# Attention and fp8 feed-forward kernel: the order of work inside a half-group stage, with the output weights split first and the key projection ahead of the block products

## What is computed

```python
h = einsum('bct,bcd->bdt', x, W1[itok])
q, k, v = rope(h @ wq), rope(h @ wk), h @ wv        # 32, 8, 8 heads
out = softmax(mask(q k^T / sqrt(128))) v            # 4 query heads share a key head
x = x + out @ wo
y = einsum('bct,bcd->bdt', x, W2[itok])
x = x + fp8_round(fp8_round(y) @ fp8_round(qweight).T + bias)
```

## Time and profile before

| | us |
|---|---|
| median of 3 runs (lowest, highest) | 740.24 (737.14, 743.44) |
| the profiled execution | 742.31 |
| its span | 740.5 |
| busy in it: PE 587.3, DVE 433.7, POOL 319.0, ACT 250.3 | |

### The profile page before, as it was taken

The page is one execution under the profiler, slowest core; times in us unless marked ns, Lnnn a source line. Parts: engine busy times, 40 slices in busy tenths (PEclk is TensorE's granted clock), DMA queues, the critical chain, the costliest instruction groups (busy, mean ns, idle before and its releaser), DMA issues.

```text
span 740.5 us, 9212 instructions
## 1 busy us (share of the span) xinstructions
PE 587.3 (79%) x3150; PEld 465.9 (63%) x3150; DVE 433.7 (59%) x660; ACT 250.3 (34%) x477; POOL 319.0 (43%) x310
## 2 busy tenths in 40 slices
PE   8988985928993899668993899289948896798992
PEld 6866863827873687547772777268736775586840
DVE  5365768635566257724772467446652686367597
ACT  3331434340426033511442052404260335042253
POOL 2074886391267408470739043922664063230001
PEclk9999988768897879868995899788987898799997
DMA  7152120103010301030011201030102001200003
GB/s 257 57 185 86 57 86 0 43 2 113 1 42 1 114 0 42 0 113 0 0 42 43 70 0 42 0 113 0 42 0 71 15 1 60 72 15 1 1 0 113
DMA packets 32644, 35.27 MB, mean 48 GB/s; under 512 B 2251, under 2 KB 22859, under 8 KB 32620
## 3 DMA queue, kind: packets, MB, share of 16 engines
q1 hardware_dynamic: 32620, 34.96, 14.7%
HBM read 28.66 MB, written 6.29 MB: 47 GB/s over the span
## 4 chain that ended last, share of the span: by engine, by line
issue 37%; PE 29%; POOL 25%; DVE 6%; DMA 2%; ACT 1%; POOLq 1%; SPq 0%; DVEq 0%; ACTq 0%
POOL wq_lo L371 9%; POOL q_rot L385 7%; PE bank L724 6%; PE bank L725 5%; PE bank L726 5%; POOL wo_lo L380 4%; PE bank L784 3%; POOL k_rot L385 1%; DVE q_swap L1041 1%; DMA values<-v_st 1%; PE bank L696 1%; PE bank L667 1%; POOL w_sum L364 1%; PE bank L698 1%; PE bank L697 1%
## 5 line engine op out<-in xcount | busy, mean ns | idle before, releaser
L385 POOL TENSOR_TENSOR q_rot<-q_rot,q_swap 128x512 f32<-128x512 f32 x64 | 85.6, 1338 | 285.9 <-DVE q_swap L1041 285.9
L724 PE MATMUL bank<-wo_hi,o_hi 128*128 128x512 f32 x256 | 111.7, 436 | 103.7 <-POOL wo_lo L380 90.9
L1089 DVE TENSOR_TENSOR xacc<-xacc,bank 128x512 f32<-128x512 f32 x64 | 43.3, 677 | 149.4 <-PE bank L726 149.4
L724 PEld LDWEIGHTS bank<-wo_hi,o_hi 128*128 128x128 f32 x256 | 52.6, 205 | 122.9 <-issue 73.6
L531 ACT ACTIVATE o_hi<-bank 128x512 fp32r<-128x512 f32 x64 | 36.0, 598 | 233.9 <-PE bank L784 233.9
L725 PE MATMUL bank<-wo_lo,o_hi 128*128 128x512 f32 x256 | 107.4, 420 | 0.0
L726 PE MATMUL bank<-wo_hi,o_lo 128*128 128x512 f32 x256 | 107.1, 418 | 0.0
L514 ACT ACTIVATE q_swap<-bank 64x512 f32<-64x512 f32 x80 | 47.6, 596 | 108.7 <-DVE bank L1021 54.9
L784 PE MATMUL bank<-p_tr,v_st 32*128 32x128 f32 x512 | 57.6, 336 | 23.1 <-DVE s_nat L1047 11.6
L1041 DVE TENSOR_TENSOR q_swap<-q_swap,cst 128x512 f32<-128x512 f32 x80 | 72.4, 905 | 0.0
L784 PEld LDWEIGHTS bank<-p_tr,v_st 32*128 32x128 f32 x512 | 53.9, 232 | 29.2 <-issue 29.2
(11 more groups left out here) (161 smaller groups left out, 1095.1 us busy)
## 6 DMA issues: line engine op xcount, KB each, us to landing
raw_q<-in_L_attn_wq SPq DMA_DIRECT2D x16, 512.0 KB, 3.9
raw_o<-in_L_attn_wo SPq DMA_DIRECT2D x8, 1024.0 KB, 6.5
v_st<-values SPq DMA_DIRECT2D x16, 256.0 KB, 4.6
xacc<-in_x SPq DMA_DIRECT2D x4, 512.0 KB, 7.2
raw_k<-in_L_attn_wk SPq DMA_DIRECT2D x8, 256.0 KB, 4.3
values<-v_st SPq DMA_DIRECT2D x8, 256.0 KB, 2.0
out<-xacc SPq DMA_DIRECT2D x8, 256.0 KB, 2.0
raw_o<-in_L_attn_wv SPq DMA_DIRECT2D x1, 1024.0 KB, 8.0
```

What stands on the lines that cost most here:

```text
L385: pool.tensor_tensor(item_out(h, k), item_out(h, k), q_swap[(h + k) % 2][:], ALU.add).then_inc(rope_done, 1)
L724: pe.matmul(dst, l_hi, r_hi, start=(i == 0), stop=False)
L1089: dve.tensor_tensor(xacc[:, tile, :], xacc[:, tile, :], w_ps[j % 2][:], ALU.add).then_inc(acc_done, 1)
```

## The change

It reorders the half on all engines. PE: attend, key, products, output tiles; the attend loop runs over batches inside, over tiles outside, and its four signals come with the last tile's matmuls. The key product stays in `a_ps`, and the first block product goes to `bank[6]`, which is also the even bank of the output projection: products wait for the previous half's accumulate 2, and the output projection for `first_kept`. The key becomes rotary item 0, the query items 1 to 4. The output weights are split first: `wo_high` 0, 1 at the start of ACT's half and 2, 3 after `keep_first`; `wo_low` 0, 1 before POOL's first rotary add, and 2, 3 after it. `q_high` 0 to 3 and `q_low` 0 to 3 come before rotary items 1 to 4, and `k_low` before `q_low` 4. DVE spreads the softmax steps between sums, puts accumulate 0 between rotary items 3 and 4, and transposes the scores at the end of `half(g, 1)`, ahead of accumulate 3. SP waits for the products in place of the key before it loads the feed-forward weights. `winograd` is renamed `block_sum`, its body kept.

```diff
 bank = [ctx.enter_context(nc.psum_tensor(f"bank{i}", [P, 512], F32)) for i in range(8)]
 a_ps, b_ps, c_ps, d_ps, e_ps, spare_ps = bank[0:6]
-product_ps = [a_ps, b_ps, c_ps, d_ps, b_ps, c_ps, e_ps]
-item_ps = [d_ps, b_ps, c_ps, e_ps, a_ps]
-k_ps = a_ps
+k_ps, one_ps = a_ps, bank[6]
+product_ps = [one_ps, b_ps, c_ps, d_ps, b_ps, c_ps, e_ps]
+item_ps = [k_ps, d_ps, b_ps, c_ps, e_ps]
...
 def item_out(h, k):
-    return k_rot[:, h, :] if k == 4 else q_rot[:, item_row[k], 2 * h + item_head[k], :]
+    return k_rot[:, h, :] if k == 0 else q_rot[:, item_row[k - 1], 2 * h + item_head[k - 1], :]

 def unit_of(g, h):
...
-    sp.wait_ge(key_mm, 2 * KV)
+    sp.wait_ge(prod_mm, PRODUCTS * 2 * KV)
...
+        if split_wo is not None:
+            wo_low(split_wo, 0, wo_lo)
+            wo_low(split_wo, 1, wo_lo)
         rope_add(g, h, 0)
-        rope_add(g, h, 1)
+        if split_wo is not None:
+            wo_low(split_wo, 2, wo_lo)
+            wo_low(split_wo, 3, wo_lo)
         if more:
-            q_low(*follow, 0)
-            q_low(*follow, 1)
-        rope_add(g, h, 2)
+            for i in range(4):
+                q_low(*follow, i)
+        for k in range(1, 5):
+            rope_add(g, h, k)
         if more:
-            q_low(*follow, 2)
-        rope_add(g, h, 3)
-        if more:
-            q_low(*follow, 3)
-        rope_add(g, h, 4)
-        if split_wo is not None:
-            for head in range(REP):
-                wo_low(split_wo, head, wo_lo)
-        if more:
+            if h == 1:
+                k_low(g + 1)
             for i in range(4, PRODUCTS):
                 q_low(*follow, i)
-            if h == 1:
-                k_low(g + 1)
...
-    def wo_high(g, hi):
+    def wo_high(g, hi, heads=range(REP)):
...
-        for head in range(REP):
+        for head in heads:
             act.activation(hi[:, head, :], raw_o[:, head, :], ACT.Copy).then_inc(wo_hi_done, 1)

     def swap(g, h, k):

         n = 5 * (2 * g + h) + k
-        if k == 4:
+        if isinstance(g, int) and n == 0:
+            act.wait_ge(t_lo_done, 4)
+        if k == 0:
             act.wait_ge(key_mm, 2 * g + h + 1)
         else:
-            act.wait_ge(sum_done, SUMS * (2 * g + h) + ITEM_SUM[k])
+            act.wait_ge(sum_done, SUMS * (2 * g + h) + ITEM_SUM[k - 1])
...
     def keep_first(g, h):
         act.wait_ge(prod_mm, PRODUCTS * (2 * g + h) + 1)
-        act.activation(first_p[:], a_ps[:], ACT.Copy).then_inc(first_kept, 1)
+        act.activation(first_p[:], one_ps[:], ACT.Copy).then_inc(first_kept, 1)

     def exponent(g, r):
...
+        if split_wo is not None:
+            wo_high(split_wo, wo_hi, range(0, 2))
         if last is not None:
-            o_high(*last, 0)
-            o_high(*last, 1)
+            for b in range(BPT):
+                o_high(*last, b)
+        swap(g, h, 0)
         keep_first(g, h)
-        if last is not None:
-            o_high(*last, 2)
-            o_high(*last, 3)
+        if split_wo is not None:
+            wo_high(split_wo, wo_hi, range(2, 4))
         if soft is not None:
             exponent(*soft)
-        swap(g, h, 0)
+        if more:
+            for i in range(4):
+                q_high(*follow, i)
         swap(g, h, 1)
-        if more:
-            q_high(*follow, 0)
-            q_high(*follow, 1)
         swap(g, h, 2)
         if more:
-            q_high(*follow, 2)
+            q_high(*follow, 4)
         swap(g, h, 3)
         if more:
-            q_high(*follow, 3)
+            q_high(*follow, 5)
         swap(g, h, 4)
-        if split_wo is not None:
-            wo_high(split_wo, wo_hi)
         if more:
-            for i in range(4, PRODUCTS):
-                q_high(*follow, i)
+            q_high(*follow, 6)
...
     def pair(g, h, last):
         n = 2 * g + h
-        if isinstance(g, int) and n == 0:
+        if isinstance(g, int) and n < 4:
             pe.wait_ge(t_lo_done, 4)
+            pe.wait_ge(v_copied, min(2 * TILES - V_LATE + 2 * n, 2 * TILES))
         else:
-            pe.wait_ge(rope_cos, 5 * n)
-            if h == 0:
-                pe.wait_ge(s_turned, 2 * g)
+            pe.wait_ge(acc_done, TPU * (2 * last[0] + last[1]) - 1)
...
     def key(g, h):
         pe.wait_ge(wk_lo_done, g + 1)
-        pe.wait_ge(first_kept, 2 * g + h + 1)
+        if isinstance(g, int) and 2 * g + h == 0:
+            pe.wait_ge(h_kept, TILES)
+            pe.wait_ge(h_lo_done, TILES)
+        else:
+            pe.wait_ge(rope_cos, 5 * (2 * g + h))
+            if h == 0:
+                pe.wait_ge(s_turned, 2 * g)
...
-        for b in range(BPT):
-            own = slice(T * b, T * (b + 1))
-            for j in range(TPU):
+        for j in range(TPU):
+            for b in range(BPT):
+                own = slice(T * b, T * (b + 1))
                 mm = pe.matmul(ps[b][:, j * P:(j + 1) * P], v_st[r][own, j, :], p_tr[own, j * REP:(j + 1) * REP, :],
                                start=True, stop=True)
-            mm.then_inc(pv_mm, 1)
+                if j == TPU - 1:
+                    mm.then_inc(pv_mm, 1)

     def project_out(g, r, j, left=(o_hi, o_lo), weights=(wo_hi, wo_lo)):
...
+        key(g, h)
         pair(g, h, last)
-        key(g, h)
+        if last is not None or fill:
+            pe.wait_ge(first_kept, n + 1)
...
-    def winograd(g, h, step):
+    def block_sum(g, h, step):
...
     def half(g, h, last=None, weights=None, fill=()):

-        if weights is not None:
-            if h == 0:
-                turn_scores(g - 1, 0)
-                turn_scores(g - 1, 1)
-            for step in range(3):
-                soft(*weights, step)
+        def soft_part(*steps):
+            if weights is not None:
+                for step in steps:
+                    soft(*weights, step)
+
+        def add_out(j):
+            if last is not None:
+                accumulate(*last, j)
+
+        soft_part(0, 1, 2)
...
-        for step in range(5):
-            winograd(g, h, step)
         rope(g, h, 0)
-        winograd(g, h, 5)
+        block_sum(g, h, 0)
+        block_sum(g, h, 1)
+        block_sum(g, h, 2)
+        soft_part(3)
+        block_sum(g, h, 3)
+        soft_part(4)
+        block_sum(g, h, 4)
         rope(g, h, 1)
-        winograd(g, h, 6)
+        block_sum(g, h, 5)
         rope(g, h, 2)
+        block_sum(g, h, 6)
         rope(g, h, 3)
+        add_out(0)
         rope(g, h, 4)
+        soft_part(5)
         for i in fill:
             v_copy(i)
-        if last is not None:
-            accumulate(*last, 0)
-        if weights is not None:
-            soft(*weights, 3)
-            soft(*weights, 4)
-        if last is not None:
-            accumulate(*last, 1)
-        if weights is not None:
-            soft(*weights, 5)
-            soft(*weights, 6)
-        if last is not None:
-            accumulate(*last, 2)
-            if not (isinstance(g, int) and 2 * g + h == 2 * KV - 1):
-                accumulate(*last, 3)
+        add_out(1)
+        soft_part(6)
+        add_out(2)
+        if h == 1:
+            turn_scores(g, 0)
+            turn_scores(g, 1)
+        if not (isinstance(g, int) and 2 * g + h == 2 * KV - 1):
+            add_out(3)
...
-    turn_scores(KV - 1, 0)
-    turn_scores(KV - 1, 1)
```

## The result

551.4 us median (551.0 to 552.86, 4 runs) beside 739.94 us of the kernel before: ratio 0.745, 95% interval 0.742 to 0.749. The forecast was 562, its range 545 to 600. The profiled execution took 551.23 us, its span is 549.4, so again 1.8 us lie around it.

The account below looks back on a forecast made before the run. PE was the bound, with the order in which other engines serve it. Opening, halves and tail summed to a 555.8 us span, 557.6 with 1.8 around it, 555.5 at the median; 6 us added gave 562, range 545 to 600.

Parts of the forecast that it names:

- The hole: PE's 13.29 us wait for the low output weights in each half(g, 1); forecast to go, with 2.9 us to spare.
- the layout: One half timed from its attend's start on all engines; a pair of halves becomes 52.4 us, from 79.1.
- my A: Attend time with loops exchanged: taken as 1.5 us, between 1.0 and the present 2.82; 17 x 1.3 = 22 us.
- the right neck: Tightest places for PE: scores behind the last rotary add, 0.6 us to spare; output tile 2 behind accumulate 0, 0.9.
- The 6 us that I added: Badly met DVE and POOL steps that exclude each other: about 0.45 us x 14 halves.
- Rival 1: Loads limit the attend, which stays at 2.8 us: 584 us, chance 0.20.
- The load rule: Attend's 128-column loads cost 0.107 us each, so nothing gained from exchanging loops; not held binding as stated.
- The half clock: PE matmuls behind stops step by 0.43 us, not 0.23; its going saves 6.9 us a pair of halves.
- rival 2: POOL and DVE late at the scores and output tile 2, half clock returns: 598 us, chance 0.15.
- the forecast's own range: 547 to 572 us, from attends of 1.0 to 1.9 us and 0 to 12 us of small stops; chance 0.59.
- Rivals 2 to 4: Includes, besides rival 2 and rival 4, the wait for output weights staying in part: about 650 us, chance 0.03.
- rival 4: Slower: PE's clock doesn't hold 2.4 GHz without pauses; at 1.2 GHz throughout about 845 us, chance 0.03.

Follow-up runs that it names:

- the second profile of the changed kernel: The changed kernel run again unchanged, on the same chip as the last edits, as their base: 549.55 us.
- The tail experiment: Changed kernel with DVE's o_low of unit (7, 0) ahead of accumulate 3 of unit (6, 1) in the tail: 545.62 us, ratio 0.737 to the kernel before.

## Why the prediction was right, point by point

*What bounds it.* PE and the others' order: yes. PE's share of the chain went from 29 to 88%.

*The hole.* Right that it goes and that 7 x 13 us hang on it: 100 us alone in the kernel before, 101 when put back. The steps of the layout can be checked in half (5, 1), whose attend starts at 330.93. POOL's rows:

```profile
332.89 3.01 POOL L380 TENSOR_TENSOR wo_lo<-raw_o,wo_hi 128x512 fp32r<-128x512 f32 x2
338.41 1.30 POOL L385 TENSOR_TENSOR k_rot<-k_rot,q_swap 128x512 f32<-128x512 f32 x1 [2.51 <-DVE q_swap L1046]
339.68 2.54 POOL L380 TENSOR_TENSOR wo_lo<-raw_o,wo_hi 128x512 fp32r<-128x512 f32 x2
...
351.29 1.68 POOL L385 TENSOR_TENSOR q_rot<-q_rot,q_swap 128x512 f32<-128x512 f32 x1 [0.63 <-DVE q_swap L1046]
```

The first two splits end 5.0 us into the half (forecast near 5), the key's add at 8.8 (8.5), the other two at 11.3 (11.0), the last rotary add at 22.0 (21.7). The scores follow it with nothing to spare:

```profile
349.20 0.68 DVE L1094 TENSOR_TENSOR xacc<-xacc,bank 128x512 f32<-128x512 f32 x1
...
353.02 1.19 PE L775 MATMUL bank<-q_rot,k_rot 128*32 128x128 f32 x36
```

They start at 353.02, the add ends at 352.97. Accumulate 0 ends at 349.88, and output tile 2 begins at 350.12. So I had the right neck; its margins are 0.05 and 0.24 us and not 0.6 and 0.9. Half of what is missing is supply: the last add and accumulate 0 come 0.34 and 0.35 us later in the half than laid out. The rest is demand: the attend is 0.4 us shorter than my A, and PE wants the add 0.2 and the accumulate 0.3 us earlier. No stop came of it.

*The sum.* The forecast is 10.6 us above the measured time. The span was laid out 6.4 us too long (555.8 for 549.4), 6 and a rounding of 0.5 came on top, and 2.3 go the other way: I took off 2.1 for a profiled execution above its median, and the profiled execution of the changed kernel lies 0.2 below its own.

*The 6 us that I added* for unlucky meetings of DVE and POOL were the largest single error. Meetings do happen (the last add takes 1.68 us and not 1.30), but they fall inside the margins, the same in each loop pass: the five pairs together took 259.24 us, 51.85 each. In this repeating schedule the meetings recur in each pass and never grow into a stop; spreading a chance over 14 halves had no row behind it.

*The attend.* A was 1.5; the time to the next matmul's start, 307.15 - 306.05, is 1.10, and 1.17 with the drain. The prediction counts 17 attends; there are 16, since only 13 of the halves have one. The 13 halves came out 4.3 us shorter together than laid out, 0.3 each, and the attend is the larger part of that. Rival 1 fell with it.

Two rules had been named for it, and the one on packing was nearer. By the Trainium skill (TensorE: Matmul & The Clock Gate, Part 3: Packing small matmuls) A was an estimated 0.9 us; the trace has 1.10. The load rule was set aside because 0.088 us an instruction lay under it. That reading was too quick, since 0.088 is an average over batches that overlap, and within one row group the steps are 0.11 us. The Trainium skill (TensorE: Matmul & The Clock Gate, section LDWEIGHTS) gives 0.107 us for a load of 128 columns. The trace's 0.11 within a row group is close to that, and its average of 0.035 over four groups shows that it is no bound on them together. Whether the load or the 128 columns of the matmul itself set the 0.11 was not told apart.

*Opening and tail.* Attend (1,1) came 3 us earlier than laid out. The scores start 1.0 later than forecast (98.26 for 97.3) but run at full clock (1.95 us; 3.17 in the earlier trace rows), so that half (1, 0) starts where it was laid out, at 101.1 for 101.3. The 3 us are in the half itself, from its first product or key matmul to attend (1,1): 19.9 us for the 22.7 forecast and the 23.7 before. DVE sets its end, as I had said, but its last rotary step there ends 18.4 us into the half for 20.4 before, and two softmax steps are left behind it where there were four. I had taken 1.0 us for what turned out to be 3.8. The ends on DVE, first in the kernel before, then in the changed one:

```profile
125.70 0.98 DVE L1041 TENSOR_TENSOR q_swap<-q_swap,cst 128x512 f32<-128x512 f32 x1
...
129.07 0.71 DVE L1076 STREAM_TRANSPOSE p_tr<-s_nat 128x512 f32<-128x512 f32 x1
```

```profile
118.84 0.68 DVE L1046 TENSOR_TENSOR q_swap<-q_swap,cst 128x512 f32<-128x512 f32 x1
119.45 0.68 DVE L1074 TENSOR_TENSOR s_nat<-s_exp,s_rec 128x512 f32<-128x512 f32 x1
120.16 0.71 DVE L1081 STREAM_TRANSPOSE p_tr<-s_nat 128x512 f32<-128x512 f32 x1
```

The tail came 0.9 later than laid out, and the cause is the clock. A stop of 3.22 us stood there before as well, and each stretch with an attend is shorter by 1.2 to 1.7 us. But behind the stop 14 matmuls now start at half clock where 6 did, and the stretch from the stop to the last attend takes 11.21 us for 9.71 (their number is not fixed: it is 12 in the second profile of the changed kernel):

```profile
669.90 0.77 PE L724 MATMUL bank<-wo_hi,o_hi 128*128 128x512 f32 x1 [3.22 <-issue]
...
679.61 0.59 PE L784 MATMUL bank<-p_tr,v_st 32*128 32x128 f32 x3
```

```profile
478.95 0.77 PE L721 MATMUL bank<-wo_hi,o_hi 128*128 128x512 f32 x1 [3.22 <-issue]
...
490.16 1.17 PE L786 MATMUL bank<-p_tr,v_st 32*128 32x128 f32 x32
```

The first two lines are from the kernel before. The tail experiment shortened this stop, and with it the half clock went.

*The half clock* was counted at 6.9 us a pair. For the sum that was right, since all of it went (1.00 in the windows). As a price of a single cause it was wrong: the run with the transposes back pays 17 us and not 32, and the kernel before with the new attend gains 40 and not 31. The prices of single edits, some measured in the kernel before and some in the changed one (100 + 27 + 17 + 15 us for split, attend, transposes and accumulate), reach 159 of 189 us, and don't have to add up. An order in which they do: the early split takes 100 us off the kernel before. Of the 89 us from there to the changed kernel, the run with the early split shows 19.4 in stops for the accumulate and 13.8 for the transposes, the 16 attends 26.4, and attend (1,1) starts 8.1 earlier. That is 67.7, and 21 are left for the clock. An estimate from the two traces agrees: 107 matmuls of 512 columns over 0.55 us there and 41 in the changed kernel, at 0.2 us each 13 us, and 7.4 us of attends at half clock. Which edit each part of these 21 belongs to is not shown.

*Slips in the sums.* By its own terms rival 2 costs 3 + 0.6 + 3.3 = 6.9 us a pair and not 6.5, so about 601 us and not 598, and the upper end of 572 for the forecast's own range would be 575. Neither touches the forecast.

*Rivals 2 to 4.* None came. The point from which rival 4 would have decided, a mean clock of two thirds, was never near: 0.972 over the run. The two falls of the clock without a stop, in the run with the old attend loop, are a small sign in its direction.

## What to carry to other kernels

When one engine stands still for another that is not slow but busy with later things, lay one stage out from the start of its first instruction, with the steps of the present trace, and look for the smallest margin: it held here to about 0.35 us in steps. Price causes together where they share a clock loss, and don't take a stop's price from a run in which another stop hides it. To see what a stop did to the clock, look at the granted clock for some microseconds behind it, and not only at the first instruction. And put small float32 matmuls with few rows in an order in which neighbours use different row groups and banks; it cost nothing visible here and gave 5% alone.

## What the runs showed of the hardware

- 32x128 float32 matmuls started 0.11 us apart within one row group in every order, and up to four row groups (each with its own bank) worked side by side: 32 instructions took 2.82 us batch by batch, 1.72 alternating over two groups and 1.17 over four.
- PE's granted clock stayed at 1.00 with PE busy without a pause over a pair of halves, 52 us.
- The same stop of 2.0 to 2.4 us for the scores was followed by half clock in six of six cases in the kernel before, in six of six with the short attend (three times only 1.1 us after PE had started again), and in three of six in the changed kernel with the transposes put back. What tells them apart was not tried.
- The clock also fell with no stop of PE before it: twice in the changed kernel with the old attend loop, behind an attend of 2.82 us (granted clock 0.57 from 210.95 to 214.90).
- Idle matmuls kept the clock up over a 7.3 us wait (32 in 7.43 us), but the gain was taken back by the next engine in line.
